# Cross-attention and a routed feed-forward: the router's logits in column halves, and new places in a hand-written order

## What is computed

```python
q, k, v = heads(layernorm(x) @ w_q), heads(context @ w_k), heads(context @ w_v)
x = x + softmax(q @ k.T * SCALE) @ v @ w_o + b_o          # per head
t = layernorm(x)                                          # 4096 tokens
gates = softmax(t @ router_w + router_b)                  # 4096 x 8
pos = cumsum(chosen, axis=0) - 1                          # place in its expert's list
valid = chosen and pos < 640
buf[e, pos] = t                                           # scatter
y = sum over e of gates * valid * (gelu(buf[e] @ w1[e] + b1[e]) @ w2[e] + b2[e])
x = x + y
```

## Time and profile before

| | |
|---|---|
| median of 3 runs | 1018.03 us (1017.87 to 1019.42) |
| profiled execution | 1018.17 us |
| its span, first to last instruction | 1016.3 us |
| busy: TensorE, DVE, ACT, POOL | 979.9, 769.2, 624.3, 284.2 us |
| TensorE's mean granted clock | 0.993 |
| attention, periods 0 to 63 | start to about 742 us |
| tail: router of the last batches, scatters, first rows | to about 768 us |
| experts | to 1016.3 us |
| TensorE busy from 300 to 400 us | 99.14 of 100 |
| TensorE busy from 720 to 740 and 740 to 760 us | 17.36 and 16.02 of 20, the warming turns included |

### The profile page before, as it was taken

One profiled execution on the slowest core, in us unless ns is written; L12 is line 12 of the kernel. 1 busy time (PEld: TensorE's weight loads), 2 busy tenths in 40 slices (PEclk: granted clock), 3 DMA queues, 4 the chain that ended last, 5 costly groups with the idle time before them and its releaser, 6 DMA issues.

```text
span 1016.3 us, 23196 instructions
## 1 busy us (share of the span) xinstructions
PE 979.9 (96%) x8382; PEld 883.9 (87%) x8382; DVE 769.2 (76%) x2088; ACT 624.3 (61%) x1736; POOL 284.2 (28%) x440
## 2 busy tenths in 40 slices
PE   7889999999999999999999999999888999999996
PEld 6778888888888888888888888888678999999996
DVE  6897768878787888878787887878755666776662
ACT  5777767777776777777676777777514333344330
POOL 5542021314223131313223131311442333222233
PEclk9999999999999999999999999999999999999998
DMA  8440101101010101101010110001105543444522
GB/s 241 144 114 2 33 2 33 43 13 55 14 40 15 33 13 33 44 2 43 12 32 6 33 35 6 17 5 50 58 18 178 137 96 80 113 128 129 136 26 26
DMA packets 48431, 56.74 MB, mean 56 GB/s; under 512 B 5324, under 2 KB 44218, under 8 KB 48192
## 3 DMA queue, kind: packets, MB, share of 16 engines
q1 hardware_dynamic: 39488, 46.30, 14.7%
q0 software_dynamic: 8832, 8.98, 5.5%
HBM read 36.01 MB, written 24.20 MB: 59 GB/s over the span
## 4 chain that ended last, share of the span: by engine, by line
PE 71%; DVE 18%; ACT 5%; issue 4%; DMA 0%; POOLq 0%; POOL 0%; another core or an unknown queue 0%; ACTq 0%
PE psum L561 29%; PE psum L756 11%; PE psum L658 8%; PE psum L644 7%; PE psum L628 7%; PE psum L672 7%; DVE prob L985 5%; ACT prob L819 3%; DVE negmax L974 3%; DVE kl L922 1%; DVE al L922 1%; PE psum L566 1%; DVE stats L929 1%; PE psum L719 1%; DVE ql L963 1%
## 5 line engine op out<-in xcount | busy, mean ns | idle before, releaser
L819 ACT ACTIVATE prob<-psum,negmax 128x256 f32<-128x256 f32 x512 | 239.1, 484 | 81.6 <-DVE negmax L974 81.6
L771 ACT ACTIVATE probt<-psum 128x512 f32<-128x512 f32 x256 | 157.6, 617 | 53.4 <-PE psum L644 51.1
L974 DVE TENSOR_REDUCE negmax<-psum 128x2 f32<-128x512 f32 x256 | 160.0, 683 | 22.0 <-PE psum L628 21.9
L985 DVE TENSOR_SCALAR prob<-prob,invtot 128x256 f32<-128x256 f32 x512 | 168.0, 392 | 4.5
L644 PE MATMUL psum<-ident,prob 128*128 128x128 f32 x1024 | 154.4, 275 | 3.3 <-DVE prob L985 1.7
L644 PEld LDWEIGHTS psum<-ident,prob 128*128 128x128 f32 x1024 | 120.5, 142 | 14.5 <-issue 4.4
L898 ACT ACTIVATE hid<-psum,b1t 128x640 f32<-128x640 f32 x64 | 50.9, 795 | 133.2 <-PE psum L561 133.2
L658 PE MATMUL psum<-probt,v 128*64 128x256 f32 x1024 | 124.6, 385 | 0.8 <-ACT probt L771 0.8
L541 POOL DMA_INDIRECT out_rows<-y,rowi x40 | 65.7, 1644 | 174.5 <-DVE y L1137 169.6
L505 POOL DMA_INDIRECT slot_table<-row,picki x64 | 64.7, 1011 | 170.2 <-DVE picki L1087 143.2
L819 ACT ACTIVATION_READ_ACCUMULATOR prob<-psum,negmax 128x1 f32 x512 | 111.2, 217 | 0.0
(11 more groups left out here) (159 smaller groups left out, 2738.4 us busy)
## 6 DMA issues: line engine op xcount, KB each, us to landing
w1r<-in_w SPq DMA_DIRECT2D x8, 1024.0 KB, 8.1
w2r<-in_w SPq DMA_DIRECT2D x8, 1024.0 KB, 10.4
slot_table<-blank SPq DMA_DIRECT2D x8, 662.5 KB, 9.8
rows<-slot_table SPq DMA_DIRECT2D x7, 662.5 KB, 5.4
xin<-in_x SPq DMA_DIRECT2D x16, 256.0 KB, 3.0
out_rows<-x SPq DMA_DIRECT2D x16, 256.0 KB, 3.2
c<-in_ctxt SPq DMA_DIRECT2D x16, 128.0 KB, 3.1
c<-in_ctxt SPq DMA_DIRECT2D x32, 64.0 KB, 2.9
```

The costliest lines, as they stand in the source:

```text
L771: copy = lambda dst, src, **kw: act.activation(dst, src, ACT.Copy, **kw)
L819: last = act.activation(prob[:, m % 2, u, qb, :], psum[:, u, qb * S:(qb + 1) * S], ACT.Exp, bias=negmax[:, m % 2, u, qb:qb + 1], accum_out ...
L974: dve.tensor_reduce(negmax[:, m % 2, u, :], psum[:, u, :].rearrange("p (q s) -> p q s", q=ST), AX.X, ALU.max, negate=True).then_inc(sem("m ...
L985: last = dve.tensor_scalar(prob[:, m % 2, u, qb, :], prob[:, m % 2, u, qb, :], invtot[:, m % 2, u, qb:qb + 1], None, ALU.mult)
```

## The change

All of it is in `timeline()` and in the stages that it names. In the order of the diff:

- **Third periods:** `slot` of an old batch stands ahead of `pv` in the list, so behind the maxima and ahead of `a_lo` on DVE.
- **Fourth periods:** `logits` stands behind `pv` and no longer between turns 2 and 3. `exp2` stands ahead of `q`, and `bias` directly behind it, one period earlier than before.
- **Logits in halves:** each matrix product of 128 token columns with the 8 router columns becomes two of 64, which write to the upper and the lower 64 partitions of the result.
- **Periods 62, 63 and the tail:** a new order. Logits, bias, shift, gate and rank of batch 13 go from 62 into 63; POOL's `w_lo` 0 and 1 become `w_rest` 0 and 1 on DVE; `o` of the last batch is cut into `o_most` (six of eight pairs, before the last `a_lo`) and a rest; scatters of batch 13 go ahead of `ln2_root` of batch 15, those of 14 behind `x2t` of 15. The row of 14 warming turns goes.
- **Banks of their own:** `x2t` and `logits` of batches 14 and 15 use banks 2, 3, 0, 1 (APART), which the scores no longer need.

```diff
--- before.py
+++ after.py
@@ timeline(), the loop over periods
         out += steps("max2 max3", m)
+        out += [("slot", b - 3)] if r == 2 and 3 <= b else []
         out += steps(pv, m - 2) if m >= 2 else []
-        if 3 <= b:
-            out += {0: [("bias", b - 3)], 2: [("slot", b - 3)]}.get(r, [])
+        if r == 3 and 2 <= b:
+            out += [("logits", b - 2)]
+        if r == 3 and 2 <= b:
+            out += [("exp2", m), ("bias", b - 2)]
...
-        out += steps("turn0 copy0", m - 1) + [("exp2", m)] + steps(k, m + 1) + steps(half[0], m)
+        out += steps("turn0 copy0", m - 1) + ([] if r == 3 and 2 <= b else [("exp2", m)]) + steps(k, m + 1)
+        out += steps(half[0], m)
...
-        if r == 3 and 2 <= b:
-            out += [("logits", b - 2)]
         out += steps("turn3 copy3", m - 1)
@@ timeline(), the last period and the tail (one piece of it)
+            *steps("turn3 copy3", m), ("slot", c), ("w_rest", 0),
+            ("o_most", ST * e), ("ln2", d), *steps("keys pick scatter", c), *steps("pv a_hi", m),
@@ banks
+APART = {("x2t", B - 2): 2, ("logits", B - 2): 3, ("x2t", B - 1): 0, ("logits", B - 1): 1}
...
+                if (stage, n) in APART:
+                    pe.wait_ge(sem("exp"), UNITS * PERIODS)
+                    pe.wait_ge(sem("probt"), UNITS * PERIODS - 1)
+                    return psum[:, APART[stage, n], :]
@@ TensorE
+            def o_most(n):
+                o(n, range(PAIRS - 2))
+
+            def o_(n):
+                o(n, range(PAIRS - 2, PAIRS) if n >= ST * (B - 1) else range(PAIRS))
...
                 for t in range(ST):
-                    mm = products(dst[:, t * NE:(t + 1) * NE],
-                                  [(x2t[:, k, t * P:(t + 1) * P], rwt[:, k, :]) for k in range(DC)])
+                    for k in range(DC):
+                        for h in range(2):
+                            r = slice(h * HD, (h + 1) * HD)
+                            mm = pe.matmul(dst[r, t * NE:(t + 1) * NE], x2t[:, k, t * P + h * HD:t * P + (h + 1) * HD],
+                                           rwt[:, k, :], start=(k == 0), stop=(k == DC - 1))
                 mm.then_inc(sem("logits"), 1)
@@ DVE
+            steps = dict(split_lo=split, ln1=ln1, xt_lo=xt, w_rest=lambda piece: split_w(0, piece), ...
```

60 lines of the change are left out of this document (35 added, 25 removed).

## The result

The kernel after takes **1015.61 us** (median of 14 runs, 1013.66 to 1017.62), the kernel before 1019.19 us (14 runs): ratio 0.9966, 95% interval [0.9958, 0.9974], 3.6 us less. The forecast was 1009.7 us, 8.3 us less. The sign is right, the size less than half. The profiled execution took 1014.67 us, 3.5 us less than before; its span is 1012.9 us.

A forecast was written before the change was run, and what follows sets the result against it. TensorE was taken to bound the attention, with real waits in third periods, period 63 and the tail. Terms -4.8 + 1.6 - 0.84 - 4.3 = -8.3 us against 1018.17 gave 1009.8, as median 1009.7; range 1004.5 to 1016.0.

The forecast's parts named there:

- Slots behind the maxima, -4.8: Third periods: slot and valid fill DVE's idle time before al, so TensorE's keys find their bank free; 4.8 us gained.
- the stated bound of 4.8: Third periods: the largest gain given for moving the slots; the smallest was 3.8 us, with 0.1 us of wait left in each.
- Logits, +1.6: 13 fourth periods: logits in halves, moved behind the products with v, lose 0.12 us each, 1.6 us in all.
- X: Fourth periods: TensorE's price for the 16 half-width logits instructions, taken as 0.45 us, bounds 0.40 to 0.90.
- turn 2 to scores: Fourth periods: time on TensorE from turn 2 to the next scores, forecast at 1.48 us, of which 0.52 is waiting.
- rival of serial halves: Fourth periods: half loads run one after the other, X = 0.90, adding 5.9 us for 1015.6; chance 0.12.
- the rival without a new wait: Fourth periods: ACT's earlier exponentials let copy 2 through, so 6.8 us less, 1002.9; chance 0.10.
- Period 62, -0.84: Period 62: logits, bias, gate and rank of batch 13 leave it and nothing takes the logits' place; 0.84 us gained.
- the slower rival: Second periods: turn 2 waits for DVE's norms; 0.85 us lost in all 13 would give 1020.7; chance 0.06.
- The tail, -4.3: Period 63 and the tail: the last scatter's issue ends at t = 43.5 instead of 47.9; 4.3 us gained, bounds 1 to 6.
- Cover: the root of batch 14; without it they cost 1.2 each: Tail: DVE's two weight-split instructions, 1.22 us each, stand where DVE waits, hidden by the root of batch 14.
- Loading the rows and the experts follow as before: After the tail: row loading and experts unchanged, 0 us, with the 90 warming turns moving along with pos of batch 15.

The follow-up runs named there:

- full_moved: Kernel after with the loop's logits at their new place but in full width, 8 instructions instead of 16: 1019.24 us, ratio 1.0055 to the kernel before.
- w_rest_again: Second run of the kernel after with VectorE's two weight remainders given back to GpSimd behind the last scatter: 1016.47 us, ratio 0.9949 to the kernel before.
- the three later traces: Kernel after with weight remainders on GpSimd (second run), with 106 warming turns (second run), and with several helpful edits combined: 1016.47, 1015.58 and 1008.88 us.
- ctx_early: Kernel after with GpSimd's split of the next context ahead of a batch's four scatters, in fourth periods: 1013.81 us, ratio 0.9999 to the kernel before.
- slots_only: Kernel before with only slots and valid of an old batch moved behind the maxima of third periods: 1013.31 us, ratio 0.9934.
- new_loop_old_tail: Loop of the kernel after, with the last two periods and the tail written as before: 1016.87 us, ratio 0.9970 to the kernel before.

## Why the prediction was half right

**Slots behind the maxima, -4.8: right** on the chip of the profile (-5.3, alone 6.5 in the medians, where the interval reaches from 5.4 to 8.2). It lies above the stated bound of 4.8, for one thing since third periods without a visible wait fell by 0.12 each too (12.66 to 12.54). What I took for a property of the program, VectorE late at `valid`, is one of the chip: with signals in time the same edit gives 1.4.

**Logits, +1.6: right**, +1.5, by its parts: X = 0.42 (0.45 forecast), turn 2 to scores 1.49 (1.48), together +0.10 a period. The rest of the 1.5 is one period, 39, that is 0.16 longer than the others. The rival of serial halves is refuted by full_moved, the rival without a new wait by the wait of 0.45 us on ACT's `probt` at 543.50.

**Period 62, -0.84: right**, -0.85.

**Second periods: the slower rival's mechanism, in four places** and not in 13, 1.7 us. In these four it goes with late landings of scatters behind instruction fetches; of `bias` no run shows a cost. It bites only where late signals had made VectorE late already: on the other chips the same landings left second periods at 9.86. The sum had left it out.

**The tail, -4.3: the term that failed.** The step that failed is "Cover: the root of batch 14; without it they cost 1.2 each". It had the cover upside down: the root is not what hides VectorE's remainder, it is what the remainder stops. By steps, on the chip of the profile:

| step, t | forecast | measured | what came in between |
|---|---|---|---|
| picki of 12 | 7.7 | 7.7 | |
| scatters of 12 landed | 14.6 | 14.7 | |
| root of 14 ends | 16.8 | 17.9 | a root step beside w1l, 1.0 longer |
| picki of 13 | 19.6 | 20.6 | |
| scatters of 13 landed | 26.5 | 28.6 | first scatter beside w1l, 1.0 longer |
| root of 15 ends | 28.7 | 30.7 | |
| bias of 15 | 32.0 | 34.6 | x2t and logits at half clock, 0.6 |
| picki of 15 | 37.9 | 40.8 | pos held by the warming turns, 0.3 |
| last issue ends | 43.5 | 46.3 | |

With the 2.0 us of the port taken off, the tail would have been forecast at -2.3; -1.9 was measured. The late signal at 727.02 is a second ceiling: it brings the statistics of 15, forecast for 25.0, to t = 26.5, and w_rest_again shows that on such chips most of the port's 2 us is waited for anyway. The half clock behind t = 28.8 was in no term of the sum.

**"Loading the rows and the experts follow as before": wrong** by 1.3 us. With the tail shorter and no gaps in the 90 turns they end 1.4 us ahead of the rows, and the granted clock falls to one half at the experts' start. The two runs with 106 turns give this back.

Sum: 2.4 from the tail, 1.3 from the clock and 1.7 from second periods are the 5 us between forecast and profile, less 0.5 that the slots gave over.

Open: the cause of the late signals beyond their place beside the third and fourth scatter; what makes most second periods long in the three later traces; what moved the instruction fetches onto the landings; and ctx_early on a chip where second periods are long.

## What to carry to other kernels

When work moves from one of VectorE and GpSimd to the other, look at what the other does at that moment: here a VectorE instruction with two inputs in SBUF, 1.22 us long, stopped GpSimd for 1.0 us, and did it twice where it was thought hidden. When a chain is shortened, count again what was tuned to its old length, here the warming turns: 1.4 and 1.0 us of idling around the rows' turns went with 3.4 us at half clock. And read the same kernel's trace on more than one chip before pricing a wait.

## What was not expected of the hardware

- TensorE's signals, 0.01 us behind their instructions elsewhere, come 0.5 to 1.7 us late around the third and fourth indirect scatter of a batch on some chips (the kernel before at 1018 to 1021 us) and in time on others (1013.6 to 1013.9 us).
- The last scatter of a batch mostly lands 1.2 to 2.0 us behind its issue's end, but 2.5 to 3.3 us where a 16 KB instruction fetch, 0.9 to 1.5 us long, starts 0.4 to 1.3 us behind that end. In all traces together that is so in 45 of 49 such places; in the other four the fetch started 0.85 to 0.88 us behind and the landing took 1.24.
- Eight matrix instructions of 8 columns in full width cost TensorE 0.88 us, and the same work as 16 column halves 0.42; a change of shape in front of them or behind adds 0.1 (turn 2 takes 0.53 instead of 0.44 ahead of halves, the products with v 1.88 instead of 1.78 ahead of full width).
- 90 warming turns took 10.0 to 12.6 us, so their end can't be counted from their number alone. At a granted clock of 1.00 and without gaps it was 10.0; gaps of 0.3 to 0.8 us in them (the kernel before, slots_only) or some microseconds at 0.50 (new_loop_old_tail, 12.6, and the kernel before on the second kind of chip, 12.0) made it longer.
